# Regrouped columns of the first node layer's sums, for side by side weight loads in the second

## The reference

```python
h = jnp.maximum(_layernorm(x), 0.0)          # nodes going in
for l in range(5):
    h = _leaky(x @ W1[l] + b1[l]) @ W2[l] + b2[l]        # node rows: 64 -> 128 -> 64
    e = _leaky(edge_attr @ We1[l] + be1[l]) @ We2[l] + be2[l]
    msg = h[src] * e * dot_scale[l]
    agg = jax.ops.segment_sum(msg, dst, num_segments=n)
    out = x + agg * res_w[l]
    x = (out - mu) * rsqrt(var + 1e-5) * ln_g[l] + ln_b[l]
# result: the first x plus this x;  _leaky has slope 0.1
```

## Time and profile before

| | |
|---|---|
| median of 3 runs | 6804.82 us (6796.08 to 6816.65) |
| profiled execution | 6786.73 us, span 6784.7 us |
| mean granted TensorE clock | 0.884 of full |
| busy: TensorE, its weight loads | 85%, 56% |
| busy: VectorE, ScalarE, GpSimd | 76%, 17%, 67% |
| L854: matmuls, weight loads | 1120 each, busy 244 and 237 us |
| L1192 on ScalarE | 148, 132 of them 128x448 |

### The profile page before, as it was taken

How to read it: one execution, slowest core, us unless ns; L and a number is a source line. 1 busy time by engine, 2 the same in 40 slices (tenths; PEclk the granted TensorE clock), 3 DMA queues, 4 the chain that set the end, 5 groups by cost and what they waited for, 6 DMA issues and landing times.

```text
span 6784.7 us, 172226 instructions
## 1 busy us (share of the span) xinstructions
PE 5734.0 (85%) x64844; PEld 3820.2 (56%) x64845; DVE 5152.1 (76%) x7991; ACT 1160.8 (17%) x1852; POOL 4527.7 (67%) x4793
## 2 busy tenths in 40 slices
PE   6776888888888888988878988887888887888887
PEld 2223443456666655666655666665566665556665
DVE  8997533588877678877758887766887775888886
ACT  0000232211111111111111111211111122111111
POOL 5777777466666457766737776754777672777775
PEclk8997566899989889999979999997999997999998
DMA  3112388755556445555635555553555563556664
GB/s 132 25 25 49 92 212 210 185 134 135 139 136 148 115 113 127 145 136 142 149 84 136 139 139 142 148 136 91 133 141 137 144 149 89 137 145 148 156 172 111
DMA packets 733557, 886.39 MB, mean 131 GB/s; under 512 B 325488, under 2 KB 502976, under 8 KB 731568
## 3 DMA queue, kind: packets, MB, share of 16 engines
q1 hardware_dynamic: 568480, 703.64, 39.7%
q0 software_dynamic: 152144, 154.93, 11.5%
q10 hardware_dynamic: 12096, 16.53, 0.8%
HBM read 749.51 MB, written 125.06 MB: 129 GB/s over the span
## 4 chain that ended last, share of the span: by engine, by line
PE 46%; issue 18%; DVE 16%; POOL 12%; DVEq 4%; ACT 3%; DMA 1%; ACTq 0%; SPq 0%; POOLq 0%
PE bank L976 14%; POOL slots L775 11%; PE bank L972 9%; PE bank L1025 7%; PE bank L1050 5%; DVE arena L1659 3%; PE bank L854 3%; PE bank L1012 3%; DVEq L1779 2%; DVE arena L1667 2%; DVE arena L1747 2%; ACT arena L1238 2%; PE bank L840 2%; DVE x_packed L1667 2%; DVE nodes_state L1715 2%
## 5 line engine op out<-in xcount | busy, mean ns | idle before, releaser
L788 POOL DMA_INDIRECT arena<-h_rows,src x3855 | 3676.5, 954 | 1798.9 <-issue 1258.4
L976 PEld LDWEIGHTS bank<-w2s,arena 128*128 128x128 f32 x8960 | 1188.5, 212 | 779.6 <-DVE arena L1747 421.8
L976 PE MATMUL bank<-w2s,arena 128*128 128x128 f32 x8960 | 1321.1, 305 | 201.0 <-DVE arena L1747 186.0
L775 POOL DMA_INDIRECT slots<-arena,slot_index x792 | 785.6, 992 | 267.1 <-issue 241.2
L972 PE MATMUL bank<-nodes_state,edge_w 64*128 64x512 f32 x980 | 617.9, 714 | 305.5 <-DVE nodes_state L1715 142.3
L1050 PEld LDWEIGHTS bank<-arena 112*64 112x64 f32 x20160 | 657.4, 141 | 269.2 <-issue 246.7
L1050 PE MATMUL bank<-arena 112*64 112x64 f32 x20160 | 744.0, 228 | 61.4 <-issue 55.3
L972 PE MATMUL bank<-x_packed,edge_w 64*128 64x512 f32 x1260 | 760.7, 686 | 16.9 <-ACT std L1187 15.9
L1238 ACT ACTIVATE arena<-bank,tenth 128x512 f32<-128x512 f32 x490 | 336.4, 687 | 2416.4 <-PE bank L972 2416.1
L1659 DVE SCALAR_TENSOR_TENSOR arena<-bank,edge_w,arena 128x512 f32<-128x512 f32 x490 | 366.6, 748 | 435.3 <-ACT arena L1238 430.4
L1667 DVE TENSOR_TENSOR x_packed<-bank,slot_rel 128x2880 f32<-128x2880 f32 (+8 forms) x315 | 588.8, 1869 | 15.9 <-issue 15.9
(11 more groups left out here) (198 smaller groups left out, 5811.7 us busy)
## 6 DMA issues: line engine op xcount, KB each, us to landing
arena<-slot_pick SPq DMA_DIRECT2D x630, 448.0 KB
arena<-h_rows SPq DMA_DIRECT2D x630, 224.0 KB
x_packed<-slot_attr SPq DMA_DIRECT2D x630, 128.0 KB
nodes_state<-attr_t SPq DMA_DIRECT2D x485, 128.0 KB
arena<-h_rows,src POOLq DMA_INDIRECT x3855
slot_pick<-arena SPq DMA_DIRECT2D x126, 448.0 KB
slots<-arena SPq DMA_DIRECT2D x9, 1904.0 KB, 22.1
arena<-slots SPq DMA_DIRECT2D x126, 136.0 KB
```

The costliest lines, as they stand in the source:

```text
L775: pool.indirect_dma_start(slots, bass.IndirectOffsetOnAxis(ap=slot_index[:, t:t + 1], axis=0), records[:, v, j, :], None).then_inc(record_ ...
L788: pool.indirect_dma_start(to[0:n, at:at + D], None, table, bass.IndirectOffsetOnAxis(ap=index[0:n, t:t + 1], axis=0)).then_inc(landed(t), 16)
L976: mm = pe.matmul(to[:, j * P:(j + 1) * P], acts[:, j * TILE:(j + 1) * TILE], w2s[:, :], start=True, stop=True)
```

## The change

ScalarE writes `y_sum` so that the columns of one product lie side by side: node 4r + s of a side goes to column s x 112 + r (2r + s in a half to s x 112 + r behind the half's start). The read in PSUM stays in order. VectorE's leaky step works column by column and stays as it is, so `y_act` has the new order too. `h` reads 112 neighbouring columns for each product. The products, their order and where they go are the same.

```diff
             def h(q, to, c=None):
                 begin, end = columns(c).start, columns(c).stop
                 sub = SUB if c is None else PSUB
+                n = (end - begin) // sub
                 for side in range(2):
                     pe.wait_ge(y_acted, upto_side(q, side, c))
                     for s in range(sub):
                         at = (side * sub + s) * D
-                        mm = pe.matmul(to[0:(end - begin) // sub, at:at + D], y_act[:, side, begin + s:end:sub],
+                        mm = pe.matmul(to[0:n, at:at + D], y_act[:, side, begin + s * n:begin + (s + 1) * n],
                                        node_w[:, H:H + D], start=True, stop=True)
                 mm.then_inc(h_ready, counts(c))
...
             def biased_side(q, of, side, c=None):
                 act.wait_ge(y_ready, upto_side(q, side, c))
-                act.activation(y_sum[:, side, columns(c)], of[:, columns(c)], ACT.Identity,
+                sub = SUB if c is None else PSUB
+                act.activation(y_sum[:, side, columns(c)].rearrange("p (s r) -> p r s", s=sub),
+                               of[:, columns(c)].rearrange("p (r s) -> p r s", s=sub), ACT.Identity,
                                bias=node_w[:, H + 2 * D:H + 2 * D + 1]).then_inc(y_biased, counts(c))
```

## The result

| | before | changed |
|---|---|---|
| median of 5 runs | 6804.82 us (6796.08 to 6816.65) | 6697.04 us (6661.36 to 6699.37) |
| ratio | | 0.9842, 95% interval 0.9815 to 0.987 |
| profiled execution | 6786.73 us | 6661.36 us, span 6659.3 us |
| mean granted clock in it | 0.884 | 0.896 |

A later group of runs gave 6674.7 against 6800.8 us, ratio 0.9826 (0.9794 to 0.9857). The forecast was 6696 us.

The account below looks back on a forecast made before the run. TensorE held 46% of the chain, with L854's strided weight loads on it in the four middle stages. 77 + 2.6 + 29 - 0 = 109 us off the 6804.8 us median gave 6696 us; 8-in-10 range 6655 to 6765.

Parts of the forecast that it names:

- The loads, at full clock: L854's sixteen weight loads, 44 tiles in the edge steps: 3.38 us becomes 1.63, gaining 77 us (67 to 108).
- the bound of 0.93 us: Lower bound for L854's sixteen loads at full clock, if only the 64 moved columns counted.
- At half clock: Two other whole tiles a layer: 3.38 us becomes 3.06, 2.6 us in all; halved last tiles gain nothing.
- That the steps can take it: VectorE's idle time (2.4 us a tile) and GpSimd's slack let the edge steps pass on the full 77 us.
- The clock: Falls behind 21 of 44 product groups cost 39 us, 0.43 per us at half clock; three quarters return, 29 us.
- ScalarE's writes: L1192's scattered writes of y_sum: 0 taken, range 0 to +0.44 us each; 112 exposed, 49 us at the most.
- The set-up: The 14 node tiles of the set-up stage lie beside GpSimd's sending of edge records, so they gain nothing.
- the clock does not come back: Rival: falls behind the products remain, gain 80 us, 6725 us; chance 0.22, shared with dearer writes.
- taken up by another wait: Rival: TensorE meets a transfer or VectorE in half of the steps, about 40 us remain, 6765 us; chance 0.05.
- the step is not what holds the loads: Rival: the address step does not slow L854, which keeps 3.38 us; 6805 us; chance 0.05.
- writes cost: Rival: L1192's writes at +0.44 us with the clock not back, gain 31 us, 6774 us; chance 0.22, shared.
- the slower one: Rival: scattered L1192 writes hold up edge activations, deciding from 0.71 us more each; at +1.30 us, 6871 us; chance 0.04.

Follow-up runs that it names:

- pairs experiment: Changed kernel, but ScalarE writes pairs of neighbouring values to scattered places and the products load every second column; ratio 0.9958 to the kernel before, on a chip where that takes 11337 us.
- writes only: Changed kernel with the products again loading every fourth column, ScalarE's writes still regrouped; ratio 0.9996 to the kernel before, on the chip where that takes 11337 us.
- first group: Four kernels, each made from the changed one by altering its loads or ScalarE's regrouping, on a chip where the kernel before took 11337 us; ratios 0.9958 to 0.9996.
- loads only: Changed kernel with ScalarE's writes in order again, loads still side by side; ratio 0.9958 to the kernel before, on the chip where that takes 11337 us.

## Why the prediction came out

**The loads, at full clock**: 1.63 us from L976 by weight columns, measured 1.65. 44 x 1.73 is 76 us for the 77. Right; the bound of 0.93 us did not come, so the 64 moved columns do not set the pace.

**At half clock**: 3.06 forecast from the halved tile, 3.06 measured, and nothing for the halved tiles themselves.

**That the steps can take it**: right, 1.70 us of 1.73 is missing from VectorE's idle time in the tile read above, and GpSimd kept its slack. Over all 44 steps nothing of the 76 us was lost: with the clock's 99 x 0.42 they make up the whole 117.

**The clock**: the mechanism was right and its size too small. All 21 falls went, not three quarters, and they were worth 41 us (29 forecast). The price of 0.43 us for each us at half clock, taken from one pair of steps, holds: 0.42 from all of them. Outside the 44 stretches nothing was gained: 667 us at half clock before, 668 in the changed kernel.

**ScalarE's writes**: the term was wrong, though its range took the cost in. I took 0 from a fill that writes pairs, over a read row that said +0.30 us and TensorE's that said +0.44. Measured +0.39 us an instruction and 26 us in all, of at most 44 (112 x 0.39). The fill was no fair neighbour: its elements stood in twos, and the pairs experiment shows on ScalarE what that is worth, 663 against 1024 ns. A read with a step of 16 bytes in PSUM took 634 ns, as in order.

The rule of the Trainium skill that the prediction weighed (Advanced Engine Details and Errata, SBUF Cachelines: two accesses to one 16-byte line, or a penalty) agrees with both numbers on writes, 1024 and 663 ns. It is stated for SBUF; for PSUM the Trainium skill (Advanced Engine Details and Errata, PSUM Cachelines) gives 8-byte lines and speaks of a slowdown of matmuls, which no run here tries.

**The set-up**: wrong. "The 14 tiles of the set-up stage lie beside GpSimd: nothing." The chain of waits led through GpSimd's sends, but what follows is the turning of the slots, which starts when node tiles and plan are done (802.6 us) and runs on until 1282 us, well behind GpSimd's last send at 1153. I had followed the chain that ended last in the stretch of the node tiles alone; the wait that held the turning was not on it. The set-up gave 28 and 13 us in two profiles of the changed kernel.

So the sum 77 + 3 + 29 - 0 + 0 = 109 met a measured 108 us with three terms off: 12 us too little for the clock, nothing for the set-up where two profiles show 13 and 28, and nothing for the writes, which took 26. That the forecast lies within 1 us of the medians' distance is luck: a second group of runs has 126 us, and the two profiled executions 125. In those two the layers are 76 + 3 + 41 - 26 = 94, measured 97, and the set-up is 28. Which part of this the median execution lacks was not profiled.

Of the rivals, "the clock does not come back" and "taken up by another wait" fell with the windows and VectorE's idle time; "the step is not what holds the loads" with writes only; "writes cost" came true beside the forecast, not in its place; the slower one was half right: its mechanism is there, at 0.39 us an instruction against the 0.71 from which it would have decided.

## What to carry to other kernels

A group of instructions whose time does not change with TensorE's clock is held by something else; compare its pace by columns with a neighbour at both clocks, and the gain can be estimated before anything is built. If data must be regrouped between two layers, do it where it is free: here in ScalarE's read of PSUM, not in its write. And a stage that the chain of waits leads around is not off the path until it is clear what its end releases.

## What was not expected of the hardware

- Float32 weight loads one to each 16 bytes: 211 ns a pair of 112 columns at either clock; one to each 8 bytes: 108 at full clock, 191 at half; side by side: 103 and 191.
- Behind a group of such slow loads, 3.38 us long, the clock fell in about half of the cases: behind 21, 25 and 24 of 44 groups in the three profiles with strided loads in the layers, none in the seven with dense ones, even at nearly the old length. In the set-up the clock was 0.50 through all node tiles with strided loads, 0.67 to 0.91 from 650 to 740 us with side by side ones. On the chip of the first group this does not separate: there the clock was below 1.00 in 27 to 32 of the 44 windows in all four kernels, and mostly so ahead of the group already.
- ScalarE, 128x448 float32: 1024 ns when each element is written 448 bytes from the last one, 663 in pairs, 633 in order; 634 when it is read with a step of 16 bytes in PSUM and written in order.
- On the chip of the first group L1194 took as long as elsewhere, but the engines were kept waiting, and the mean granted clock was 0.717 in loads only where the first profile of the kernel before has 0.884. Between these two profiles GpSimd's wait for source indices came to 4006 us against 228, and the weight loads of the source rows (L1050 before, L1051 there) stood still for 1062 us against 247 where the profile shows no wait. What is slow on that chip was not tried, and stays open.
